# Dense build of a graph kernel: register loads and their range checks moved on SyncE, TensorE and ScalarE

## The reference, cut to what matters

```python
edge_index = jnp.stack([src, dst])
h = jnp.maximum(_layernorm(x, axis=-1), 0.0)
x = x + _L0_gnn_ref(h, edge_index, ...)   # softmax over the edges of a target
...
x = x + _L3_gnn_ref(h, edge_index, ...)   # segment_sum(h[row] * norm[:, None], col)
```

## Time and profile before

| | us |
|---|---|
| median of 3 runs | 7815.13 (7807.52 to 7820.11) |
| the profiled execution | 7823.92 |
| its span, first to last instruction | 7822.3 |
| `dense_tiles`, from 1308 to 2265 of the span | 957 |

### The profile page before, as it was taken

How to read it: one execution, slowest core, us unless ns; L and a number is a source line. 1 busy time by engine, 2 the same in 40 slices (tenths; PEclk the granted TensorE clock), 3 DMA queues, 4 the chain that set the end, 5 groups by cost and what they waited for, 6 DMA issues and landing times. The chain is left out here.

```text
span 7822.3 us, 163512 instructions
## 1 busy us (share of the span) xinstructions
PE 5661.5 (72%) x45916; PEld 4604.4 (59%) x45917; DVE 5021.0 (64%) x12810; ACT 3071.7 (39%) x7533; POOL 4010.7 (51%) x3849
## 2 busy tenths in 40 slices
PE   2222226665548787799999958898996899899587
PEld 2222213555448787667777746777774677777477
DVE  7444445977658677645545546778887678778622
ACT  1111101566648677544444433333333333333200
POOL 3777761677730000077777705666663666666200
PEclk9999999866669999899999978999997899999788
DMA  4111123222224233255555623444445444444456
GB/s 183 53 52 53 53 87 120 77 97 99 96 77 168 102 127 141 80 146 144 146 145 145 127 39 111 118 117 119 119 118 62 116 116 122 116 118 120 46 211 219
DMA packets 655256, 880.68 MB, mean 113 GB/s; under 512 B 305163, under 2 KB 487738, under 8 KB 636152
## 3 DMA queue, kind: packets, MB, share of 16 engines
q1 hardware_dynamic: 453512, 592.31, 23.6%
q0 software_dynamic: 119568, 245.10, 14.2%
q10 hardware_dynamic: 82000, 40.97, 1.7%
HBM read 645.04 MB, written 232.98 MB: 112 GB/s over the span
## 5 line engine op out<-in xcount | busy, mean ns | idle before, releaser
L1062 POOL DMA_INDIRECT rows<-source_table_heads,idxb x1760 | 1692.6, 962 | 853.7 <-issue 483.7
L1861 DVE TENSOR_REDUCE gtop<-ps_top 128x2 f32<-128x1024 f32 x880 | 1036.9, 1220 | 182.2 <-PE ps_top L1974 178.3
L1062 POOL DMA_INDIRECT rows<-source_table,idxb x880 | 879.8, 1000 | 351.7 <-issue 285.0
L362 POOL DMA_INDIRECT records<-recb,idxb x784 | 763.2, 973 | 256.0 <-issue 247.4
L783 PE MATMUL ps_cells<-hot 128*128 128x128 bf16 x4608 | 556.0, 268 | 372.1 <-SPq L830 265.8
L1939 PE MATMUL ps_e<-ident,rows 128*128 128x128 f32 x3520 | 544.1, 302 | 176.3 <-issue 107.2
L783 PEld LDWEIGHTS ps_cells<-hot 128*128 128x128 bf16 x4608 | 405.8, 121 | 444.8 <-issue 434.3
L1051 POOL MEMSET acc<- 128x3400 f32 x3 | 8.8, 2932 | 1261.9 <-POOLq L68 1261.9
L390 PE MATMUL ps_g<-hott 64*128 64x128 bf16 x784 | 101.0, 308 | 719.3 <-ACT hott L406 715.2
L1168 PE MATMUL ps_acc<-rows,pt 128*128 128x131 f32 x3750 | 528.2, 282 | 81.6 <-ACT pt L1215 79.2
L1939 PEld LDWEIGHTS ps_e<-ident,rows 128*128 128x128 f32 x3520 | 465.2, 206 | 183.2 <-issue 111.5
(11 more groups left out here) (333 smaller groups left out, 13851.8 us busy)
## 6 DMA issues: line engine op xcount, KB each, us to landing
logs<-log_counts SPq DMA_DIRECT2D x75, 1600.0 KB
hot<-target_rows SPq DMA_DIRECT2D x440, 256.0 KB, 2.7
wt<-edge_weights SPq DMA_DIRECT2D x50, 1600.0 KB
target_rows<-hot SPq DMA_DIRECT2D x220, 256.0 KB
hott<-target_columns SPq DMA_DIRECT2D x440, 128.0 KB
edge_weights<-both ACTq DMA_DIRECT2D x125, 320.0 KB
log_counts<-none POOLq DMA_DIRECT2D x125, 320.0 KB, 2.5
records<-blank SPq DMA_DIRECT2D x16, 1870.0 KB
```

The costliest lines, as they stand in the source:

```text
L362: g.indirect_dma_start(out=recs[:, :], out_offset=bass.IndirectOffsetOnAxis(ap=idxb[k][:, t:t + 1], axis=0), in_=recb[k][:, t, :], in_offs ...
L1062: g.indirect_dma_start(out=rows[r][:, k, :], out_offset=None, in_=table, in_offset=bass.IndirectOffsetOnAxis(ap=idxb[r][:, k:k + 1], axis= ...
L1861: ve.tensor_reduce(gtop[:, 2 * half:2 * half + 2], ps_top[:, 2 * half:2 * half + 2, :], AX.X, ALU.max) \
```

## The change

- **SyncE.** The loop runs over four batches instead of one. It loads 16 numbers of `until` at once. They are declared without run-time bounds, and each is checked apart, one ahead of the wait that uses it: the check of number j + 1 stands before the wait for number j.
- **TensorE.** The loop runs over four batches instead of two. The 16 numbers of the first of them are loaded ahead of it as before; those of the other three are loaded in the middle of the batch before, behind the wait for the third group's grant and ahead of that group's matmuls. The two tables take turns in registers.
- **ScalarE.** The numbers of `last` of the next run are loaded at the end of the last cell of a run (the instruction's place among the others is the same as before, between the clearing of the fourth bank and the wait for the next run's first cell). Only the first of the five is checked there; each of the others is checked behind the cell before, ahead of the wait that uses it.

No arithmetic on tiles changes, nor does any DMA.

```diff
--- before.py
+++ after.py
@@ -766,24 +766,31 @@
                     for r in range(RUN):
                         ins = pe.matmul(ps[:, r, :], zero[:, 0:P], zero[:, :], start=True, stop=True)
                     ins.then_inc(opened, 1)
-                    with pe.Fori(0, BATCHES // 2) as i:
-                        for k in range(2):
-                            n = 2 * i + k
-                            _, turn = nc.values_load_multi_w_load_instructions(
-                                c.turn[0:1, bass.ds(n * PB, PB)], engines=[pe.engine], min_val=0, max_val=RUN - 1,
-                                skip_runtime_bounds_check_because="a cell's number modulo RUN")
+                    def numbers(n):
+
+                        _, turn = nc.values_load_multi_w_load_instructions(
+                            c.turn[0:1, bass.ds(n * PB, PB)], engines=[pe.engine], min_val=0, max_val=RUN - 1,
+                            skip_runtime_bounds_check_because="a cell's number modulo RUN")
+                        return turn
+                    with pe.Fori(0, BATCHES // 4) as i:
+                        turn = numbers(4 * i)
+                        for u in range(4):
+                            n, k = 4 * i + u, u % 2
                             pe.wait_ge(hot_ready, n + 1)
                             pe.sem_inc(begun, 1)
                             for j in range(PB):
                                 if j % 4 == 0:
                                     pe.wait_ge(granted, n * (PB // 4) + (j // 4 + 1))
                                     pe.sem_inc(begun, 1)
+                                if j == PB // 2 and u < 3:
+                                    following = numbers(n + 1)
                                 tile = ps[:, bass.ds(turn[j], 1), :].rearrange("p a f -> p (a f)")
                                 for m in range(2, 5):
                                     pe.matmul(tile[:, 0:P], hot[k][:, 0, j // 2, :, j % 2], hot[k][:, m, j // 2, :, j % 2], start=False, stop=m == 4,
                                               skip_group_check=True)
                                 pe.matmul(tile[:, P:2 * P], hot[k][:, 1, j // 2, :, j % 2], hot[k][:, 0, j // 2, :, j % 2], start=False, stop=True,
                                           skip_group_check=True).then_inc(paired, 1)
+                            turn = following
 
                 @block.scalar
                 def _(act):
@@ -803,30 +810,47 @@
                             act.dma_start(rows_w[:, bass.ds(b, 1), r, :].rearrange("p o (q f) -> p (o q) f", f=P),
                                           both[r][:, :, 0, :]).then_inc(sums_out[r], 16)
                             act.activation(logs[r][:, :, :], both[r][:, :, 1, :], ACT.Ln, bias=tiny[:, 0:1]).then_inc(logged[r], 1)
+
+                        def ends(u):
+
+                            _, last = nc.values_load_multi_w_load_instructions(
+                                c.last[0:1, bass.ds(b * CELLS + u, RUN)], engines=[act.engine], min_val=0, max_val=PAIRS,
+                                skip_runtime_bounds_check_because="checked one by one below")
+                            return last
+                        checked = lambda q: nc.s_assert_within(last[q], min_val=1, max_val=PAIRS)
+                        last = ends(0)
+                        end = checked(0)
                         for u in range(CELLS):
                             r, q = divmod(u, RUN)
                             if q == 0:
-                                _, last = nc.values_load_multi_w_load_instructions(
-                                    c.last[0:1, bass.ds(b * CELLS + u, RUN)], engines=[act.engine], min_val=1, max_val=PAIRS)
                                 act.wait_ge(sums_out[r], b * 16)
                                 act.wait_ge(masked[r], b)
-                            act.wait_ge(paired, last[q])
+                            act.wait_ge(paired, end)
                             act.activation(both[r][:, q, :, :].rearrange("p a f -> p (a f)"), ps[:, q, 0:2 * P], ACT.Copy) \
                                 .then_inc(copied, 1)
                             if u > 0:
                                 clear(u - 1)
                                 if q == 0:
                                     log(r - 1)
+                            if q == RUN - 1 and u + 1 < CELLS:
+                                last = ends(u + 1)
+                            if u + 1 < CELLS:
+                                end = checked((u + 1) % RUN)
                         clear(CELLS - 1)
                         log(CELLS // RUN - 1)
 
                 @block.sync
                 def _(sp):
-                    with sp.Fori(0, BATCHES) as n:
+                    QUADS = PB // 4 * 4
+                    with sp.Fori(0, BATCHES // 4) as n:
                         _, until = nc.values_load_multi_w_load_instructions(
-                            c.until[0:1, bass.ds(n * (PB // 4), PB // 4)], engines=[sp.engine], min_val=1, max_val=NB * CELLS)
-                        for j in range(PB // 4):
-                            sp.wait_ge(cleared, until[j])
+                            c.until[0:1, bass.ds(n * QUADS, QUADS)], engines=[sp.engine], min_val=0, max_val=NB * CELLS,
+                            skip_runtime_bounds_check_because="checked one by one below")
+                        checked = lambda j: nc.s_assert_within(until[j], min_val=1, max_val=NB * CELLS)
+                        ahead = checked(0)
+                        for j in range(QUADS):
+                            least, ahead = ahead, checked(j + 1) if j + 1 < QUADS else None
+                            sp.wait_ge(cleared, least)
                             sp.sem_inc(granted, 1)
                     for r in range(CELLS // RUN):
                         sp.wait_ge(sums_out[r], 16 * NB)
```

## The result

The changed kernel takes 7767.5 us (7758.0 to 7773.2), the kernel before 7817.6 in the same comparison: 0.9936 of it, with a 95% interval of 0.9919 to 0.9953. That is 50 us less, where 22 were forecast. The profiled execution took 7771.0 us against 7823.9, 52.9 less.

The account below looks back on a forecast made before the run. No engine was full; a chain of waits going round the engines was taken as the bound. ScalarE -49, TensorE's borders -35, middle +59 and +5, branches -2 gave -22 us: 7815.1 to 7793, 8-in-10 range 7764 to 7824.

Parts of the forecast that it names:

- ScalarE's reload, 1.03 us shorter: At ScalarE's reload between runs, one cheaper check behind the load instead of five saves 1.03 us; the load stays 1.12 us.
- The four moved checks cost nothing: ScalarE's other four checks run while ACT copies and clears; without that cover they would give back 0.48 us per run.
- ScalarE's share, -49 us: 59 reloads on the chain of waits at 1.03 us are 61 us at most; 0.8 of it taken.
- TensorE's part beside ScalarE's, +27 us (59 + 5 - 35 - 2): Middle load behind the grant +59, further batches coming onto the chain +5, borders without load -35, fewer branches -2 us.
- One load moved for one load: In stretch one (large cells, 1308 to 1500 us), moving TensorE's load from border to middle wins nothing.
- TensorE's longer loop, nothing: Dense PE's loop grows from 256 to 512 loads and matmuls per turn; no further fetch stall was counted.
- SyncE, nothing: SyncE's turn, 1.7 us with 16 numbers (load taken at 1.1), stays hidden: nothing won, nothing lost.
- The floor of 7771: If the old chain kept its course, -61 - 40 - 2 + 59 = -44 us; hardly below 7771 unless the middle load is hidden.
- rival 1: The two halves cancel: chain turns to PE, ACT waits for pairs, shorter reloads worth half; +2 us, 7817; chance 0.27.
- rival 2: Slower: all 38 middle loads of stretch three, behind the grant, get onto the chain; +33 us, 7848; chance 0.09.
- rival 3: Middle load hidden because PE's matmuls are queued far enough ahead; -86 us, 7729; chance 0.07.
- rival 5: GpSimd becomes the bound if stretch three loses over its 67 us of idle time for logarithms; chance 0.02.

Follow-up runs that it names:

- e1: ScalarE's part of the change alone, TensorE and SyncE as in the kernel before: build 875.0 us against 946.1, ratio to before 0.9916.
- e6: e1 with all five of ScalarE's cheaper checks behind the load instead of one: build 903.1 us, 28.1 longer than e1, ratio to before 0.9961.
- e3: SyncE's part alone (16 numbers per load), against the kernel before: build 946.9 us, median +0.2 us, ratio 1.0002.
- e9: TensorE's and SyncE's parts together, ScalarE as in the kernel before: build 994.4 us, ratio to before 1.0057.
- e5: The whole change, with TensorE's middle load ahead of the wait for the grant: build 874.5 us, 27.8 shorter than the change, ratio to before 0.9919.
- e7: e1 with ScalarE's load moved right behind the logarithm, a run ahead: build 883.2 us, 8.2 longer than e1, ratio to before 0.9934.

## Why the prediction was right, and where it was off

The direction and the two mechanisms hold, and the median of 7767.5 lies in the range (7764 to 7824), 3.5 us above its lower end. The size was less than half, -22 of -50. In the build, where the whole change stands, it was -22 of -43.8, and with e1 as ScalarE's part this difference is that of ScalarE's term. By its steps:

- **ScalarE's reload, 1.03 us shorter:** right, 1.99 to 0.97 us. **The four moved checks cost nothing:** right. In all 500 cells that have their check behind the cell before, the check has ended before ACT's last instruction ahead of the copy ends, in after and in e1 alike; in the place where nothing covers them they cost 28.1 us (e6 less e1).
- **ScalarE's share, -49 us:** this is the term that was mis-sized; e1 measured -71.1. It counted the 59 reloads on one chain of before and took 0.8 of these, 38% of the 125. What arrived was 55%, and 76% in B. So reloads off that chain weren't worthless. The likely reason, read and not tested: ACT and PE take turns at being late by a few tenths of a microsecond, and a reload that is just off the chain is back on it as soon as its neighbours are shorter. The prediction itself had the row for this (true waits of 0.27 us) and used it only as a discount.
- **TensorE's part beside ScalarE's, +27 us (59 + 5 - 35 - 2):** measured +27.3 with SyncE's part and 24.1 without it, but partly by luck. The net cost was put into stretch three and none into stretch one. It came as 14.2 in A, 14.1 in B and -0.8 in C. By the spacing of the 384 waits for a grant, up to block 14, after against e1: 61 batches (46 of them with the load moved) lose 48.5 us at the border, 1.05 per load where 1.2 was taken, and gain 57.7 in front of the fourth group, 1.25 per load, just the 1.25 taken. Another 12.2 and 6.8 us appear at the second and third group: PE is earlier there and waits for its grant. That follow-up wait is a piece that the sum did not have. In stretch one there is another. In the first 25 batches, after against e1, a group with the load typically takes 2.54 us instead of 1.27 (27.4 us more for all 19), and a border without it 1.3 less (23.4 for 18), as forecast; but the six borders that keep their load grow by 4.0 us together (4.99 us instead of 3.22 at the first of them). There PE waits for `hot` (3.69 us, at 1344.73): VectorE, busy 180 of 192 us, may refill a buffer only when the batch that read it is done. The load at the border ran behind a batch's last matmul and did not delay that; the one in the middle does. VectorE's waits for TensorE between 1316 and 1500 are 7.1 us before, 4.1 in e1 and 12.2 after. "One load moved for one load" is true of the loads, and not of the grants and of the buffers behind them. No run with a third buffer tests this.
- **By itself TensorE's part costs 48.2,** not 27: when ACT is slow, the border gives back less (41.8 instead of 48.5 us up to block 14), and in C there is no GpSimd to hide the rest.
- **TensorE's longer loop, nothing:** right. The branch, whole build of after, against the earlier trace rows:

```profile
L775 PEldq COMPARE_BRANCH  x24: 76/208/222, 1340.9 to 2218.1; - x24
```

The same 208 ns at the median, and 222 at most, with 512 loads and matmuls in the loop, and the next register instruction begins at most 0.11 us behind it, as before. By the Trainium skill (Runtime: NRT & Kernel Launch, "Instruction fetch mechanics") a taken branch to a target outside the window of two pages of 256 instructions stalls for a fetch; no such stall is in the row. But the same section gives TensorE a memory for 2048 instructions, more than this loop has, so these rows don't tell whether the rule holds where it applies.
- **SyncE, nothing:** right in e3 (+0.2 us) and e9 (0.1 us of build); beside both others 3.2 us of build. Its load of 16 is 1.23 us where 1.1 was taken.
- **The floor of 7771** ("the new time can hardly be below") was 44 us less than before. The median is 50 less (37 to 63 by the interval) and the build 43.8, so the change itself doesn't show the floor broken. But its first term does not hold: it had 61 us at most for ScalarE's part, and e1's build lost 71.1.

The rivals. The two halves don't cancel (rival 1), though the rest of the change takes 27 of ScalarE's 71. The load behind the grant (rival 2) is real, as e5 shows with 27.8 us, yet far from outweighing. The middle load isn't hidden (rival 3): 1.45 us of gap at the full clock. The Trainium skill (Advanced Engine Details and Errata, "Engine Queue Depths") gives TensorE a queue of 64; what the rows show of queued work is the 0.76 us that the gap is shorter at 1.2 GHz. GpSimd (rival 5) had 0.02 and was to bind from a loss of 67 us in stretch three. It does bind in e1 and e5, and earlier than that: its waits of 57 us (to 2150) are used up when the stretch has lost 44, because its own instruction L725 grew from 2716 to 2890 ns, 14 us over 82 runs.

Of the signs named for the profile after, the reload's gap, the borders at 0.34, the gap in the middle and the shift from grants to "issue" came as written. Stretch one was to keep its time within 4 us and needed 6.3 more for its 400 pairs; stretch two made up for it. Stretch three was to lose 15 to 35 us and lost 43. "I am wrong if ACT's wait for pairs grows by as much as its reloads shrink": in blocks 0 to 6 it did (25.5 us against 19.7), in blocks 7 to 23 by half (30.0 against 59.3).

What stays open: the granted clock of 1630 to 2150 rose from 0.65 to 0.70 in after and e5, and to 0.68 in e1. The clock does not set the order of the kernels: after and e5 have the same 0.70 and differ by 27.8 us of build, and e1 with 0.68 is as short as e5. How much of the gain is the clock's, and how much of the clock's rise is the gain's, these runs don't separate. Nor is it settled why GpSimd's L725 takes longer.

The best versions are e1 and e5, 66 us faster than before: ScalarE's part with TensorE's load either left at the border, or moved ahead of the wait. Against the change they are 27 us shorter by the build, and 16 us by the medians of two comparisons, whose intervals overlap.

## What to carry to other kernels

A load into registers that can't be dropped should stand ahead of a wait that is long anyway; behind the wait its length is added to what follows (here 28 us of build by the order of two lines). And a load that stood between two batches delays a buffer's release once it stands within one. When a gain per turn is certain and two engines take turns at being late, count more of the turns than one chain of waits goes through: 38% were taken, 55% came in all and 76% in B. Before pricing a gain, look for the engine with the next smallest idle time and add up its waits: that sum, less what its instructions grow, is where the gain ends.

## What the hardware showed that was not expected

- **Loading registers costs by their number, and on ScalarE more than that.** TensorE's 16 take 1.11 us, SyncE's 4 and 16 take 0.30 and 1.23. ScalarE's 5 take 0.54 us at the least and 1.13 at the median; its 25 take 1.94 at the least and 6.44 at the median. A further register costs 0.07 us on ScalarE by the difference of the shortest, and 0.06 (by the shortest) to 0.08 us (by the medians) on SyncE; what makes 25 of them take over three times as long on ScalarE in most blocks, these runs don't tell.
- **ScalarE's load is longer behind a running logarithm** (1.75 us at the median of 74 in e7 and of 24 before) than behind a copy or a table load (1.12 and 1.13), so the logarithm's 0.83 us gave no cover here.
- **TensorE's load is longer in the middle of a batch at times:** 2.02 us at 1980.2 us in after, with a gap of 2.15; the mean over the 96 loads is 1.33 us there and 1.20 before, at the same median.
